# Layer stage of a decoder kernel: one norm chain on ScalarE as Ln and Exp, six table operations on GpSimd, and new orders

## The reference, cut to what matters

```python
for i in range(6):
    x = attn_layer(shift_tokens(x), Wqkv[i], q_scale[i], k_scale[i], Wo[i]) + x
    x = ffn_layer(shift_tokens(x), ln_g[i], ln_b[i], W1[i], b1[i], W2[i], b2[i]) + x

# attn_layer: 16 heads of 64, window 32
q, k, v = split(x @ Wqkv)
q = q / max(norm(q), 1e-12) * q_scale          # per head
k = k / max(norm(k), 1e-12) * k_scale
q = q * cos * scale + rotate_half(q) * sin * scale
k = k * cos / scale + rotate_half(k) * sin / scale
out = local_attention(q, k, v) @ Wo            # softmax(8 q k^T, banded causal mask) v
# ffn_layer: layer norm, then (a * gelu(gate)) @ W2 + b2 with a, gate = split(x @ W1 + b1)
```

## Time and profile before

| | us |
|---|---|
| median of 3 runs | 4329.48 (4317.6 to 4334.51) |
| the profiled execution's own time | 4337.59 |
| its span, first to last instruction | 4335.7 |
| PE busy | 4129.3 (95%) |
| DVE busy | 3657.2 (84%) |
| ACT busy | 3374.8 (78%) |
| POOL busy | 2644.3 (61%) |

### The profile page before, as it was taken

One profiled execution on the slowest core, in us unless ns is written; L12 is line 12 of the kernel. 1 busy time (PEld: TensorE's weight loads), 2 busy tenths in 40 slices (PEclk: granted clock), 3 DMA queues, 4 the chain that ended last, 5 costly groups with the idle time before them and its releaser, 6 DMA issues.

```text
span 4335.7 us, 150399 instructions
## 1 busy us (share of the span) xinstructions
PE 4129.3 (95%) x61520; PEld 3085.9 (71%) x61520; DVE 3657.2 (84%) x11101; ACT 3374.8 (78%) x9585; POOL 2644.3 (61%) x2210
## 2 busy tenths in 40 slices
PE   7999989999999999999999999999999789999999
PEld 5777756666666666666666666666666578888888
DVE  4665699999999999999999999999999567766766
ACT  3455478989999899989999899989999556566665
POOL 3444477777777777767777777777777333333331
PEclk9888899999999999999999999999999889999999
DMA  3000000000000000000000000000000100000000
GB/s 103 4 4 4 5 2 4 4 4 4 29 5 3 4 29 4 4 4 3 29 5 4 4 29 4 4 4 9 26 9 9 29 2 4 4 4 4 4 4 7
DMA packets 65257, 46.42 MB, mean 11 GB/s; under 512 B 29220, under 2 KB 63032, under 8 KB 63800
## 3 DMA queue, kind: packets, MB, share of 16 engines
q1 hardware_dynamic: 64568, 36.78, 3.0%
HBM read 28.48 MB, written 2.10 MB: 7 GB/s over the span
## 4 chain that ended last, share of the span: by engine, by line
PE 74%; DVE 14%; ACT 8%; issue 2%; POOL 1%; SPq 0%; DMA 0%; DVEq 0%; POOLq 0%; ACTq 0%
PE ps L570 61%; PE ps L574 14%; DVE BIG L1133 5%; ACT BIG L922 4%; ACT BIG L914 4%; DVE sm L1144 3%; DVE BIG L1141 1%; POOL BIG L1594 1%; DVE BIG L1138 1%; DVE sm L1141 1%; ACT ps L914 1%; DVE BIG L1137 1%; DVE BIG L1211 0%; DVE sm L1133 0%; DVE x_sb L1133 0%
## 5 line engine op out<-in xcount | busy, mean ns | idle before, releaser
L570 PE MATMUL ps<-WB,BIG 128*128 128x128 f32 (+2 forms) x8576 | 1959.9, 365 | 64.6 <-DVE BIG L1141 46.1
L914 ACT ACTIVATE BIG<-ps 128x512 f32<-128x512 f32 (+5 forms) x3168 | 1440.8, 513 | 517.5 <-PE ps L574 337.9
L1594 POOL TENSOR_TENSOR BIG<-BIG,sm 128x512 f32<-128x512 f32 (+1 forms) x864 | 1223.1, 1425 | 700.3 <-DVE sm L1345 517.5
L570 PEld LDWEIGHTS ps<-WB,BIG 128*128 128x128 f32 (+1 forms) x8576 | 1142.3, 192 | 349.2 <-issue 178.0
L1594 POOL TENSOR_TENSOR BIG<-BIG 128x512 f32<-128x512 f32 x768 | 966.3, 1279 | 92.4 <-DVE BIG L1133 92.3
L574 PEld LDWEIGHTS ps<-t_ident,BIG 128*128 128x128 f32 x6016 | 725.8, 146 | 355.9 <-issue 232.6
L574 PE MATMUL ps<-t_ident,BIG 128*128 128x128 f32 x6016 | 915.9, 283 | 53.6 <-DVE BIG L1133 24.1
L1144 DVE TENSOR_REDUCE sm<-BIG 128x8 f32<-128x512 f32 (+3 forms) x1472 | 880.8, 615 | 36.1 <-ACT BIG L922 33.4
L570 PEld LDWEIGHTS ps<-BIG 64*64 64x64 f32 (+2 forms) x37888 | 629.7, 131 | 347.4 <-issue 159.7
L570 PE MATMUL ps<-BIG 64*64 64x64 f32 (+4 forms) x37888 | 767.0, 226 | 70.4 <-ACT ps L914 20.3
L1597 POOL TENSOR_TENSOR sm<-sm,halfn 128x1 f32<-128x1 f32 (+2 forms) x336 | 290.5, 871 | 750.2 <-DVE sm L1137 418.2
(11 more groups left out here) (121 smaller groups left out, 3037.6 us busy)
## 6 DMA issues: line engine op xcount, KB each, us to landing
WB<-in_Wqkv SPq DMA_DIRECT2D x6, 1536.0 KB, 7.1
XS<-y_sb SPq DMA_DIRECT2D x96, 63.0 KB
y_sb<-in_ctx SPq DMA_DIRECT2D x16, 256.0 KB, 3.3
WB<-in_Wo SPq DMA_DIRECT2D x6, 512.0 KB, 8.6
x_sb<-in_x SPq DMA_DIRECT2D x8, 256.0 KB, 5.0
WB<-in_F_W SPq DMA_DIRECT2D x1, 2048.0 KB, 8.9
WB<-in_F_W SPq DMA_DIRECT2D x8, 256.0 KB, 4.9
out<-x_sb SPq DMA_DIRECT2D x8, 256.0 KB, 2.3
```

Of the source, the lines that this page charges most:

```text
L570: return te.matmul(o, l, r, start=start, stop=stop, skip_group_check=not check)
L914: return se.activation(o, i, ACT.Copy)
L1594: return pe_.tensor_tensor(o, a, b, op)
```

## The change

On DVE the nine instructions `n0` to `n8` become one, `n`, which only keeps the sum from zero. Two new ACT phases, `e` (Ln) and `h` (Exp with scale -0.5), give the inverse root; POOL's `n0 n1` wait for `h`. The rotary tables are made by POOL, one multiply at a time, at the first POOL phase of tiles 24 to 29 of a layer. ACT's table loads are written out by `table`, which emits a load where the set changes; the first stands ahead of ACT's first wait. The four strings of `C_ORDER` are new, and so are `SLOT["c"]` and `BEGIN` of two stages.

```diff
-    "pe": "1b06 1a06 2g26 2a26 1v06 1b16 2a18 2g16 1a16 1y8 1q14 1k04 1x3 1v15 2tr5 1s6 1p07 2g07 1k14 1o8 1p17 "
-          "2o8 2a07 1q03",
+    "pe": "1a05 1b05 1o8 1a15 2o8 1p07 1q13 1b15 1p17 1x2 1k03 2g07 1s5 2g25 2a25 1y7 1v14 2tr4 2a17 2g15 2a07 "
+          "1k13 1v05 1q02",
...
-SLOT = {"ab": 14.8, "c": 11.6, "de": 25.4}
+SLOT = {"ab": 14.8, "c": 11.38, "de": 25.4}
...
-    "c": {"pe": 469.1, "act": 460.6, "dve": 471.2, "pool": 459.6},
-    "de": {"pe": 3302.5, "act": 3287.2, "dve": 3283.2, "pool": 3316.1},
+    "c": {"pe": 488.7, "act": 467.7, "dve": 477.3, "pool": 465.7},
+    "de": {"pe": 3257.7, "act": 3236.3, "dve": 3238.1, "pool": 3251.8},
...
+            loaded = [None]
+
+            def table(name):
+
+                if loaded[0] != name:
+                    se.preload_act_table_set(name)
+                    loaded[0] = name
+
+            table("natural_log_exp_and_others")
             w.wait_ge("k_a", 16 * len(SETS["a"]))
...
+                elif ph == "e":
+                    table("natural_log_exp_and_others")
+                    w.wait_ge(*u.on("dve", "n"))
+                    o = act(sm_[u.at["t"] % 4][:, 5, 0:32], sm_[u.at["t"] % 4][:, 2, 0:32], ACT.Ln)
+                elif ph == "h":
+                    table("natural_log_exp_and_others")
+                    w.wait_ge(*u.on("act", "e"))
+                    o = act(sm_[u.at["t"] % 4][:, 5, 0:32], sm_[u.at["t"] % 4][:, 5, 0:32], ACT.Exp, scale=-0.5)
                 elif ph[0] == "s":
+                    table("natural_log_exp_and_others")
...
+                    table("gelu_and_others")
...
                 elif ph[0] == "n":
-                    i = int(ph[1:])
-                    if i == 0:
-                        for m in ("r0", "r1", "l0", "l1"):
-                            w.wait_ge(*u.on("dve", m))
-                        o = stt(sm[:, 2, 0:32], sm[:, 1, 0:32], 1e-24, sm[:, 1, 0:32], ALU.max, ALU.max)
-                    else:
-                        o = newton(u, sm[:, 5, 0:32], sm[:, 2, 0:32], sm[:, 6, 0:32], i - 1)
+                    for m in ("r0", "r1", "l0", "l1"):
+                        w.wait_ge(*u.on("dve", m))
+                    o = ts(sm[:, 2, 0:32], sm[:, 1, 0:32], 1e-24, None, ALU.max)
...
+            def rope_table(l, i):
...
+                qsv = WB[:, OQS:OQS + 128].rearrange("p (a d) -> p a d", a=2)
+                a, n = i // 3, i % 3
+                if n == 0:
+                    o = tt(rc[:, l % 2, a, :], T["rotc"][:, 64 * a:64 * a + 64], qsv[:, a, :], ALU.mult)
+                else:
+                    c = 32 * (n - 1)
+                    o = tt(rs[:, l % 2, a, c:c + 32], T["rots"][:, 64 * a + c:64 * a + c + 32], qsv[:, a, 32 - c:64 - c], ALU.mult)
+                o.then_inc(sems["rope"], 1)
...
             def pool_c1(u, ph):
...
+                if ph == u.marks["pool"][0]:
+                    for i in range(6 if l + t == 0 else 0):
+                        rope_table(0, i)
+                    if 0 <= t - NT + 8 < 6 and l + 1 < depth:
+                        rope_table(l + 1, t - NT + 8)
...
-                    w.wait_ge(*u.on("dve", "n8"))
+                    w.wait_ge(*u.on("act", "h"))
```

More of the change, by code:

```diff
@@ L976, in act_c1 @@
                 b = c_bufs(u, int(h) if h in "01" else 0)
-                K = bank[u.bank[{"o": "y", "f": "s"}.get(ph[0], ph[0]) + ph[1:]]]
+                K = None if ph in "eh" else bank[u.bank[{"o": "y", "f": "s"}.get(ph[0], ph[0]) + ph[1:]]]
                 two, three, four = before(u, 2), before(u, 3), before(u, 4)
@@ L1060, in act_de @@
                 t, b, sm = u.at["t"], de_bufs(u), de_bufs(u).sm
+                if ph in ("e0", "e1", "g1", "g2", "ex", "em", "x3"):
+                    table("natural_log_exp_and_others")
                 K = bank[u.bank[ph]] if ph in u.bank else None
@@ L1245, in dve_ab @@
                 o.then_inc(u.name("dve", ph, sems), 1)
-            def rope_tables(l):
-                w.wait_ge("wq", 16 * (l + 1))
-                w.wait_ge("k_c", 16 * len(SETS["c"]))
-                if l >= 2:
-                    for m in ("q0", "q1", "k0", "k1"):
-                        w.wait_ge(*uC1[(l - 2, NT - 1)].on("dve", m))
-                qsv = WB[:, OQS:OQS + 128].rearrange("p (a d) -> p a d", a=2)
-                for a in range(2):
-                    tt(rc[:, l % 2, a, :], T["rotc"][:, 64 * a:64 * a + 64], qsv[:, a, :], ALU.mult).then_inc(sems["rope"], 1)
-                    for h in range(2):
-                        tt(rs[:, l % 2, a, 32 * h:32 * h + 32], T["rots"][:, 64 * a + 32 * h:64 * a + 32 * h + 32],
-                           qsv[:, a, 32 - 32 * h:64 - 32 * h], ALU.mult).then_inc(sems["rope"], 1)
             def newton(u, o, a, t, i):
@@ L1280, in dve_c1 @@
                 sm = sm_[t % 4]
-                if (l == 0 and t == 0 or t == NT - 2 and l + 1 < depth) and ph == u.marks["dve"][0]:
-                    rope_tables(l + (t > 0))
                 if ph in NORM:
@@ L1632, in pool_ab @@
                 o.then_inc(u.name("pool", ph, sems), 1)
+            def rope_table(l, i):
+                if i == 0:
+                    w.wait_ge("wq", 16 * (l + 1))
+                    w.wait_ge("k_c", 16 * len(SETS["c"]))
+                    if l >= 2:
+                        for m in ("q0", "q1", "k0", "k1"):
+                            w.wait_ge(*uC1[(l - 2, NT - 1)].on("dve", m))
+                qsv = WB[:, OQS:OQS + 128].rearrange("p (a d) -> p a d", a=2)
[6 more added lines that the diff above has]
+                o.then_inc(sems["rope"], 1)
             def pool_c1(u, ph):
-                t, h = u.at["t"], ph[-1]
+                l, t, h = u.at["l"], u.at["t"], ph[-1]
                 sm = sm_[t % 4]
+                if ph == u.marks["pool"][0]:
[3 more added lines that the diff above has]
+                        rope_table(l + 1, t - NT + 8)
                 if ph == "d":
```

5 lines of the change are left out of this document (removed), and 10 rows, old and new, of the table C_ORDER.

## The result

The kernel before took 4330.3 us in this comparison (4317.6 to 4334.5, four runs), the changed one 4297.5 (4288.9 to 4299.4, four runs). The ratio is 0.993, 95% interval 0.991 to 0.995: 33 us, 0.8% faster. The forecast was 4256, 73 us. Sign right, size under half, inside the range.

A forecast was written before the change was run, and what follows sets the result against it. PE and DVE, both within 2 us of the 58.3 us group, were taken as the bound. Layers 1 to 5 give 36, first inner layer 19, layer ends 17, start 1.3: 73 us, 4329.5 to 4256, range 4198 to 4325.

The forecast's parts named there:

- the highest need plus 1.7: Six-layer stage: a group lasts 1.7 us longer than its fullest engine needs, so 55.7 on PE gives 57.4.
- That DVE counts is seen twice: DVE helps set the period: first inner layer's groups are 1.5 us longer, those at a layer's end 4.7 longer.
- merged stretches: PE's small products: 144 of 384 stretches merge with another, 3 a group at 0.2 us each, saving 0.6 a group.
- TensorE's need: PE's work in a group if never late: from 56.3 us to 55.7.
- The group: Distance between rows of the once-a-group ACT instruction: 58.3 us to 57.4 in layers 1 to 5, saving 36 over 40 groups.
- ScalarE's need: ACT's work in a group: 51.3 us plus 1.2 for Ln and Exp and 2.9 for two loads, 55.4.
- rival 1: ACT takes DVE's place in full, groups stay at 58.2 us; 4295, or 4312 if layer ends return too; chance 20%.
- The first inner layer: Its eight groups were to fall from 59.8 us to 57.4, saving 19.
- Layer ends: Rotary tables leave DVE for POOL: 17 of the 21 us that five layer ends cost were to go.
- The seam: Joins between the layer stage and its neighbours: taken as zero, with 10 us either way.
- The drain: Wait ahead of an ACT table load: 0.15 us read from the trace, against some 1380 ns by the skill's rule.
- three signs by which the forecast would be wrong: PE's waits after table loads as long as the load; Ln rows waiting for DVE; POOL's ACT waits becoming PE's POOL waits.

The follow-up runs named there:

- a_small_apart: Changed kernel with one 512-column product moved between the two stretches of small products, so that most no longer merge; 4308.7 us, ratio 0.993 against the kernel before.
- a_less_pe: Changed kernel with six of the eight products of each tile's output projection, 1.7 us a group less for TensorE; 4299.3 us, ratio 0.991 against the kernel before.
- b_no_newton: Kernel before without the eight Newton instructions of the norm on VectorE, old orders kept, nothing added to ScalarE; 4337.7 us, one run.
- b_two_more_loads: Kernel before with two more table loads a group on ScalarE, ahead of the third Gelu, nothing else; 4434.2 us, one run.
- a_less_both: Changed kernel with Identity for Gelu (no table loads in the layer stage) and six of eight output-projection products; 4264.1 us, one run.
- a_no_loads: Changed kernel with Identity in place of the Gelus, so no table load in the layer stage; 4287.0 us, ratio 0.987 against the kernel before.
- a_short_max: Changed kernel with VectorE's row maximum taken over 32 of the 64 columns of each head; 4256.7 us, one run.
- b_rope_pool: Kernel before with only the rotary tables moved from VectorE to GpSimd, one operation a tile; 4303.2 us, ratio 0.995 against the kernel before.
- a_both_links: Changed kernel without table loads in the layer stage (Identity for Gelu) and with the row maximum over 32 of 64 columns; 4253.1 us, one run.
- a_seam_8: Changed kernel with the layer stage's lists put 8 us earlier against those of the stage ahead; 4287.6 us, ratio 0.989 against the kernel before.

## Why the prediction was right in sign and wrong in size

- **The step that failed** is the rule that the period is the highest need plus 1.7 ("So the same 1.7 is what I take: 57.4 a group"), and under it "That DVE counts is seen twice". By it the 0.9 us a group were 0.6 from merged stretches of TensorE (56.3 to 55.7) and 0.3 from VectorE's need falling below TensorE's, and the first inner layer was to fall as far. In ordinary groups neither shows: taking two thirds of the mergers back leaves the group at 57.7 (a_small_apart), 1.7 us less of TensorE's need gives 0.1 (a_less_pe), and VectorE relieved alone leaves every ordinary group at 58.3 (b_no_newton). Both observations on DVE were true (first inner layer, layer ends) and both were local: there DVE's time stood on the loop, elsewhere not. The rule is also refuted by b_two_more_loads (+2.3 for an engine that stands idle 4 us a group) and by a_less_both against a_no_loads (57.1 in both, although the highest need fell by 1.7). In its place the runs show loops through several engines, on which the row maximum stands (a_short_max, 0.5) and the loads in part (a_no_loads, 0.6 of 5.7).
- **The group**, 57.4 forecast, is 57.8. What brought it from 58.3 is not the relief. In the old orders the norm's move made it 60.5; the new orders bring this to 57.8, and they in turn can't carry nine instructions on DVE in one piece at that place. So the half us a group is that of the pair; the new orders with the norm elsewhere on DVE were not run. In the medians 20 of the 33 us come with the rotary tables alone.
- **ScalarE's need**: 55.4 forecast. With 1.4 us of waits it fills 57.8 to 56.4. The added terms were nearly right (8 x 0.12 = 1.0 for 1.2; a load with its drain 1.43 at the lone Gelu, 0.2 more behind a Ln and a copy). The 51.3 I started from was about 1 too low: 7.0 us "free" stood against 4.4 seen as waits for PE, less than the "four fifths" of rival 1, and part of the rest was work, not room.
- **The first inner layer**, 19 forecast: 8 measured. Its groups are 58.6, not 57.4, and the higher figure of before stood in five intervals, not eight. a_no_loads leaves these groups at 58.6 and a_short_max brings them to 57.7, so a loop through the row maximum holds them too.
- **Layer ends**, 17: 20 at the four ends in b_rope_pool and 16 in its stage, 21 at the ends in the trace of the change.
- **TensorE's need**: 55.7 forecast, near 55.5 read in the new timeline (but see a_both_links). Its fall gave nothing (a_less_pe, a_small_apart).
- **The seam**, taken as zero: the way from the last product of the stage before to the first of these rows grew by 7 us (161.1 to 167.8), made good in part by an earlier end of that stage and 5 us at the end of the kernel. How much of the 7 is the order isn't shown: the granted clock on this way was 0.94 before and 0.90 after, and 0.94 again in a_seam_8, which took 163.1.
- **The drain** of the rule of the Trainium skill ("ScalarE: Activation LUTs", "What ACT_TABLE_LOAD costs"), 1380 ns, doesn't show in this stream: ahead of the load at 1113.90 stand 0.36 us beyond the copy's 0.48, ahead of the one at 1115.90 0.14 beyond the Gelu's 0.57, and behind each the next instruction starts after 1.29.
- **The rivals**: rival 1 (ScalarE in DVE's place, 4295 to 4312) is the number that came, 4297.5, and ACT's half of the chain speaks for it; but a_no_loads shows that 5.7 us less of ACT give 0.6, so it isn't ACT's need that sets the group either. Its sum had other parts, too: groups of 58.2, where 57.8 came, and nothing around the stage; the meeting of the numbers is in part luck. Of the three signs by which the forecast would be wrong none appeared (no row of Ln waits for DVE, PE's longest wait for ACT in the window is 0.6 us): they looked for added costs, and what failed was the gain.

What remains open: which loop holds 57.1 and 56.4. The levels lie so close (57.8, 57.1, 56.8, 56.4) that each cut seems to uncover the next. Of the first I can name the links (copies, score product, row maximum, exponentials); of these the row maximum was cut by itself, the others are read from the chain. At 56.8 the chain is 99% TensorE's.

## What to carry to other kernels

When several engines are above 90%, don't read the period as the fullest engine's need plus a constant. Ask which chain leads from one engine to another and back, and price an edit by whether it stands on that chain; an instruction on it costs its time even on an engine with 9 us of waits, one off it is free. Try the relief alone first (leave the work out, keep the orders): one trace would have shown that it is worth nothing in an ordinary group, and one set of runs with the tables alone would have shown where most of the gain in the medians lay. An order and the placement of work are tuned as one.
